# A decoder layer in FP32: the SyncE queue re-ordered, projections and the first output projection moved to other slices

## The chip, the cores and the metric

The kernel runs on one core of one Trainium2 chip. The metric is the device time of one execution in microseconds (us). A change of half a per cent is about what a measurement of this kernel can tell from none.

## What is computed

One pre-norm decoder layer, FP32, four batches of 512 tokens, hidden size 512. The attention has 32 query heads and 8 key and value heads of 16 columns; the feed-forward part has 1792 inner columns.

```python
def bitnet_linear(x, weight, scale_param):
    s = jnp.maximum(jnp.mean(jnp.abs(weight), axis=1), 1e-08)
    y = jnp.einsum('bsi,oi->bso', x, jnp.sign(weight / s[:, None])) * (s * scale_param)[None, None, :]
    return jnp.nan_to_num(y, nan=0.0, posinf=1000000.0, neginf=-1000000.0)
# attention: q, k, v = bitnet_linear(x, ...), softmax(q k^T / 4) v, then bitnet_linear(..., o_weight, o_scale)
# FFN weights: W = mean_w + mean(|w - mean_w|) * sign(w - mean_w);  h = silu(x W1^T) * (x W3^T);  h W2^T
x = x + attention(layernorm(x))
x = x + ffn(layernorm(x))
```

## The kernel before

Every engine has its program written out by hand, and the engines meet at semaphores only. FP32 accuracy comes from splitting each operand into a high and a low FP32R part. The work has three parts.

**Attention** (lines 1321 to 1328 for PE). There are 32 *groups*, one for each batch and key head, and each group has four *slices* (`kt`, 128 keys each), so a batch is 32 slices. One slice of PE (`pe_slice`) is four shifted score products (L1254, one for each query head of the group, 50 rows: 48 of split queries and 2 of the "shift", the row maxima taken off before the exponential), two plain score tiles (L1238) 14 tiles ahead whose row maxima DVE takes (`maxima`, L973), and the values product of the slice before (L1264). ACT takes the exponentials (L813). In slice 1 PE transposes the maxima of the next group (L1244), DVE splits them (`split_shift`, L981 and L983), and SP writes them by DMA into two rows of each half of that group's `q_slot` (`load_shift`, L436). The first product of the next group waits for that (`shift_in`, L1250).

**Work beside it.** Groups of batch b also make the queries, keys and values of batch b+1: token statistics (DVE L898), normalising (POOL L620), transposes (PE L1176), a split (POOL L628, L630), six *items* of eight matmuls (`project_item`, L1184 and L1185), scaling (ACT L747), guards for infinities (POOL L641, L642, DVE L942), a second split (POOL L650, L652) and the store to DRAM (SP `store_item`, L395 to L398). `beside` says which slice has which piece, and it takes a bank of the ring of three PSUM banks (`RING3`) that the shifted scores use. The 14 tiles of each FFN weight are also loaded (`load_difference`), subtracted on POOL (L658), signed on ACT and summed in absolute value on DVE (L1069), one tile each 8 slices.

**The queue of SP** sets when transfers start. `sp_group(g)` issues in this order: the item stores due, the load of group g+3 (`load_group`), the shift rows of group g+1, a tile of differences, tokens, and last the store of the values of group g-1. SP waits at the first instruction that isn't ready, with all others behind it. Before the loop SP stores batch 0's items, loads groups 0 to 2, writes the output factors to DRAM element by element (L423), waits for that, reads them back (L426), and then issues the shift rows of group 0.

**The last groups** hold batch 0's output projection: reciprocals of the softmax sums (L988) in group 28, the scaled attention output (L994) in group 30, its split (L998), and four tiles `project` (L1275, L1276) with `residual` on DVE (L1010 to L1023, eight instructions a tile) in slices 2 and 3 of group 30 and 0 and 1 of group 31. Then follow `second_norm` (L1028 to L1034), 14 tiles of weights (DVE L1100, PE L1339, ACT L839), and the FFN of the four batches, in which the output projections of batches 1 to 3 are interleaved.

## Time and profile before

| what | us |
|---|---|
| three runs, median (lowest to highest) | 1076.51 (1076.15 to 1081.52) |
| the profiled execution's own time | 1076.51 |
| its span, first to last instruction | 1074.7 |
| start of the attention loop on PE | 78.4 |
| end of its last values product | 536.9 |
| first weight transpose | 544.8 |
| first FFN matmul | 580.5 |
| PE busy in the span | 967.8 (90%) |
| DVE, ACT, POOL busy | 748.9, 520.1, 243.0 |

The page gives busy time for each engine. A wait row says which engine and line sat idle until which other one released it. PE is busy nearly all of the time, yet a PE that waits in a queue of matmuls can count as busy, so the waits and the timeline of a stage say more than the share.

### The profile page before, as it was taken

What the parts mean: (1) busy time and instruction counts of PE and PEld (TensorE: products, weight loads), DVE (VectorE), ACT (ScalarE), POOL (GpSimd) and SP (SyncE); (2) the same over time, 40 slices, a digit from 0 to 9 for tenths busy, and PEclk for the clock granted to TensorE, in tenths of its full rate; (3) what the DMA queues carried; (4) which work ended last, traced back from release to release, by engine and by line L of the source; (5) the groups of instructions that cost most, each with busy time, mean ns of one, the idle gap of its engine ahead of it and who ended that gap; (6) DMA issues with size and microseconds to landing.
All of it is one profiled execution on the core that took longest, in us unless ns stands there. A gap on an engine that the chain in (4) does not pass through costs nothing.

```text
span 1074.7 us, 14205 instructions
## 1 busy us (share of the span) xinstructions
PE 967.8 (90%) x4770; PEld 617.4 (57%) x4770; DVE 748.9 (70%) x1020; ACT 520.1 (48%) x957; POOL 243.0 (23%) x231
## 2 busy tenths in 40 slices
PE   3548997899889988997968999999999999999997
PEld 2413443244333443332456888888888888888886
DVE  5469776987788757996786457865588456864443
ACT  3407775887578756886556232233313332232221
POOL 2004573366517552200000110101101010011110
PEclk9758998999889987997889999999999999999999
DMA  4565456445545365524457100231002400040001
GB/s 155 143 136 162 149 179 202 127 127 172 174 138 150 103 195 153 146 67 142 138 171 235 60 1 1 79 112 49 0 0 87 152 0 0 14 143 1 0 0 39
DMA packets 82257, 110.24 MB, mean 103 GB/s; under 512 B 11040, under 2 KB 34592, under 8 KB 82208
## 3 DMA queue, kind: packets, MB, share of 16 engines
q1 hardware_dynamic: 80048, 108.04, 33.1%
q10 hardware_dynamic: 2160, 1.58, 0.5%
q8 instruction: 27, 0.44, 0.2%
q14 instruction: 22, 0.18, 0.1%
HBM read 76.29 MB, written 32.78 MB: 101 GB/s over the span
## 4 chain that ended last, share of the span: by engine, by line
PE 67%; DVE 15%; DMA 8%; SPq 6%; issue 2%; ACT 2%; POOL 0%; DVEq 0%
PE psum L1349 14%; PE psum L1350 14%; PE psum L1351 14%; DVE nmx L973 8%; PE psum L1254 6%; PE psum L1264 6%; PE psum L1238 3%; DMA q_slot<-shift 3%; SPq L436 2%; PE psum L1184 1%; DMA factors<-wstat 1%; PE psum L1185 1%; DMA q_stack<-q_lo 1%; PE psum L1275 1%; PE psum L1276 1%
## 5 line engine op out<-in xcount | busy, mean ns | idle before, releaser
L973 DVE TENSOR_REDUCE nmx<-psum 128x2 f32<-128x1024 f32 x256 | 301.9, 1216 | 94.8 <-PE psum L1238 94.6
L813 ACT ACTIVATE probs<-psum 128x512 f32<-128x512 f32 x512 | 273.5, 603 | 104.8 <-PE psum L1254 103.7
L1254 PE MATMUL psum<-q_slot,k_slot 50*128 50x512 f32 x512 | 173.5, 499 | 35.0 <-DMA q_slot<-shift 32.9
L1349 PE MATMUL psum<-fxh,wh 128*128 128x512 f32 x448 | 175.2, 391 | 2.2 <-DVE wl L1111 2.2
L1350 PE MATMUL psum<-fxl,wh 128*128 128x512 f32 x448 | 175.2, 391 | 0.0
L1351 PE MATMUL psum<-fxh,wl 128*128 128x512 f32 x448 | 174.8, 390 | 0.0
L1254 PEld LDWEIGHTS psum<-q_slot,k_slot 50*128 50x128 f32 x512 | 76.0, 197 | 156.4 <-ACT probs L813 92.4
L697 POOL CAST dh<-w2T 128x512 fp32r<-128x512 f32 (+1 forms) x56 | 51.0, 912 | 430.7 <-PE psum L1351 393.5
L1264 PE MATMUL psum<-probs,v_slot 128*32 128x512 f32 x1024 | 147.2, 649 | 0.7 <-ACT probs L813 0.7
L1238 PE MATMUL psum<-k_slot,q_slot 48*128 48x512 f32 x512 | 114.6, 469 | 22.1 <-DVE nmx L973 20.6
L1118 DVE TENSOR_TENSOR gate<-gate,psum 128x512 f32<-128x512 f32 x56 | 38.4, 686 | 133.6 <-PE psum L1351 131.3
L866 ACT ACTIVATE hh<-gate 128x512 fp32r<-128x512 f32 x56 | 35.4, 632 | 162.3 <-DVE gate L1118 162.3
L863 ACT ACTIVATE gate<-psum 128x512 f32<-128x512 f32 x56 | 33.5, 599 | 164.0 <-PE psum L1351 164.0
L1349 PEld LDWEIGHTS psum<-fxh,wh 128*128 128x128 f32 x448 | 84.5, 189 | 20.9 <-issue 2.9
L1351 PEld LDWEIGHTS psum<-fxh,wl 128*128 128x128 f32 x448 | 84.5, 189 | 17.7
L1350 PEld LDWEIGHTS psum<-fxl,wh 128*128 128x128 f32 x448 | 84.4, 188 | 17.6
L1238 PEld LDWEIGHTS psum<-k_slot,q_slot 48*128 48x128 f32 x512 | 57.7, 208 | 54.0 <-DVE nmx L973 44.4
L1349 PE MATMUL psum<-dh,hh 128*128 128x512 f32 x224 | 88.2, 394 | 0.1
L1350 PE MATMUL psum<-dl,hh 128*128 128x512 f32 x224 | 88.2, 394 | 0.0
L1351 PE MATMUL psum<-dh,hl 128*128 128x512 f32 x224 | 87.1, 389 | 0.0
L1120 DVE TENSOR_TENSOR hl<-gate,hh 128x512 fp32r<-128x512 f32 x56 | 38.8, 692 | 39.8 <-ACT hh L866 39.8
L658 POOL TENSOR_TENSOR stage<-stage 128x1536 f32<-128x1536 f32 x14 | 48.6, 3471 | 36.5 <-DMA stage<-in_L_ffn_mean_w_dram 36.5
(107 smaller groups left out, 1209.3 us busy)
## 6 DMA issues: line engine op xcount, KB each, us to landing
stage<-in_L_ffn_mean_w_dram SPq DMA_DIRECT2D x84, 256.0 KB, 4.6
q_slot<-q_stack SPq DMA_DIRECT2D x64, 192.0 KB, 4.4
stage<-in_L_ffn_w_dram SPq DMA_DIRECT2D x42, 256.0 KB, 3.1
q_stack<-q_hi SPq DMA_DIRECT2D x32, 256.0 KB
weighted_values<-u_sb SPq DMA_DIRECT2D x32, 256.0 KB, 5.1
k_slot<-k_stack SPq DMA_DIRECT2D x64, 96.0 KB, 4.4
xn<-_attn_hidden_states_dram SPq DMA_DIRECT2D x4, 1024.0 KB, 5.7
q_stack<-q_lo SPq DMA_DIRECT2D x16, 256.0 KB
```

What stands on the lines that cost most here:

```text
L658: nc.gpsimd.tensor_tensor(wn[e % 2][:], wn[e % 2][:], mn[e % 2][:], ALU.subtract).then_inc(fd_ok, 1)
L697: nc.gpsimd.tensor_copy(dh[parity][:], w2T[:, bass.ds(src, 1), :].rearrange("p o c -> p (o c)")).then_inc(dh_ok, 1)
L813: nc.scalar.activation(probs[kt][:, j, :], BANK[ring_bank(("score", g, kt, j))], ACT.Exp, scale=HEAD_DIM ** -0.5).then_inc(exp_ok, 1)
L973: v.tensor_reduce(column, pair, AX.X, ALU.max, negate=True).then_inc(s_max, 1)
L1118: v.tensor_tensor(gate[:], gate[:], BANK[UP], ALU.mult).then_inc(h_ok, 1)
L1120: v.tensor_tensor(hl[p][:], gate[:], hh[p][:].bitcast(FP32), ALU.subtract).then_inc(hl_ok, 1)
L1238: last = mm(BANK[2 * jj + h], q_slot[s][rows, jj, q * P:(q + 1) * P], k_slot[s][rows, :], start=True, stop=True)
L1254: mm(BANK[ring_bank(("score", g, kt, j))], k_slot[s][rows, kt * P:(kt + 1) * P], q_slot[s][rows, jj, :], start=True, stop=True).then_inc(t ...
L1264: last = mm(psum[32 * j:32 * j + 32, 6, :], v_slot[g % 2][:, kt, :], probs[kt][:, j, :], start=(kt == 0), stop=(kt == TT - 1))
L1349: mm(o, lhs_hi, rhs_hi, start=first, stop=False)
L1350: mm(o, lhs_hi, rhs_lo, start=False, stop=False)
L1351: return mm(o, lhs_lo, rhs_hi, start=False, stop=final)
```

## The change

- SP, in each group: the shift rows of group g+1 come first, then the load of group g+3, then the values of group g-1, then the item stores, tokens and differences. The shift rows of both halves go in one DMA for each part, two a group where there were four.
- SP, before the loop: the shift rows of group 0 stand right after the third item store; the load of group 2 and the last two item stores follow. The factors are written in group 3 and read back in group 5.
- Work of batch b+1: transposes in slices 0 to 3 (8 to 11 before), items in slices 5, 8, ... 20 (13, 15, ... 23 before), values in 24 (28). Statistics and normalising are made one batch earlier; those of batch 1 stand ahead of the loop. The transposed tokens go back into `xn`, so that the two `xT` buffers and ACT's wait for them are gone.
- Batch 0's output projection: SP loads its operands from group 24, DVE scales them in slices 10 to 15 of the last batch, and a PE tile stands in slices 16, 20, 24 and 28, in a ring bank. `residual` is cut in three pieces, in the three slices that follow. PE no longer waits for the weights' coefficient in the loop.
- POOL fills the value slots two groups ahead, with three slots where there were two.
- The sums of absolute differences stay on DVE.

```diff
-STATS_AT, AGGR_AT, NORM_AT, XT_AT, SPLIT_AT = 0, 4, 5, 8, 9
-ITEM_AT = tuple(13 + 2 * i for i in range(len(ITEMS)))
-GUARD_LAG, PRED_LAG = 1, 4
-VT_AT = 28
+XT_AT, SPLIT_AT, STATS_AT, AGGR_AT = 0, 1, 12, 16
+NORM_AT = (24, 26, 28, 30)
+ITEM_AT = tuple(5 + 3 * i for i in range(len(ITEMS)))
+GUARD_LAG, PRED_LAG = 1, 3
+VT_AT = 24
+INVERT_AT, ATTENDED_AT, PROJECT_AT, PROJECT_EVERY = 4, 10, 16, 4
...
+V_SLOTS = 3
...
-        xT = [sb(f"xT{p}", [P, SEQ]) for p in range(2)]
...
-    SUMS_STEP = (0, 3)
-    ATTENDED_STEP = (2, 0)
-    SPLIT_STEP = (2, 1)
-    MEANS_STEP = (2, 1)
-    PROJECT_STEPS = [(2, 2), (2, 3), (3, 0), (3, 1)]
+    TOTALS_SLICE, MEANS_SLICE, COEFF_SLICE = 119, 121, 122
...
         if b == BATCH:
-            return None
+            t = (at - PROJECT_AT) // PROJECT_EVERY
+            return ("project", t) if at in range(PROJECT_AT, SLICES, PROJECT_EVERY) else None
...
-        store_item(0, 3)
-        store_item(0, 4)
-        group_stored(2)
-        load_group(sp, 2, 2, slot_in[2])
-        sp.wait_ge(wstat_ok, 5)
-        sp.dma_start(fac_dram.rearrange("a w p -> p a w"), wstat[:, 3:5, :],
-                     allow_slow_non_contiguous=True).then_inc(fac_out, 16)
-        sp.wait_ge(fac_out, 16)
...
         def load_shift(g, s):
             for part, ready in enumerate((sh_hi, sh_lo)):
+                r = ROWS + part
                 sp.wait_ge(ready, g + 1)
-                for h in range(2):
-                    r = HALF * h + ROWS + part
-                    sp.dma_start(q_slot[s][r:r + 1].bitcast(FP32).rearrange("o j (t c) -> o (j t) c", c=P),
-                                 shift[s % 2][8 * h:8 * h + 8, part, :].bitcast(FP32)).then_inc(shift_in[s], 16)
+                sp.dma_start(q_slot[s][r:P:HALF].bitcast(FP32).rearrange("h j (t c) -> h (j t) c", c=P),
+                             shift[s % 2][:, part, :].bitcast(FP32)).then_inc(shift_in[s], 16)
...
         load_shift(0, 0)
+        group_stored(2)
+        load_group(sp, 2, 2, slot_in[2])
+        store_item(0, 3)
+        store_item(0, 4)
...
         def sp_group(g):
...
-            if b + 1 < BATCH:
-                for i in range(5):
-                    if at <= ITEM_AT[i] + 6 < at + 4:
-                        store_item(b + 1, i)
+            if g < LAST_G:
+                load_shift(g + 1, (s + 1) % 4)
             if g + 3 < GROUPS:
                 positive(sp, t_mm, 16 * g)
                 group_stored(g + 3)
                 load_group(sp, g + 3, (s + 3) % 4, slot_in[(s + 3) % 4])
-            if g < LAST_G:
-                load_shift(g + 1, (s + 1) % 4)
+            if g > 0:
+                store_values(g - 1, s + 3)
+            if b + 1 < BATCH:
+                for i in range(5):
+                    if at <= ITEM_AT[i] + PRED_LAG + 3 < at + 4:
+                        store_item(b + 1, i)
...
+            if g == 3:
+                load_factors()
+            if g == 5:
+                spread_factors()
-            if last and s == 0:
+            if b == BATCH - 1 and at == 0:
                 for p in range(2):
                     sp.wait_ge(u_out[p], 16 * KV_HEADS // 2)
                 load_sums(0)
+                sp.wait_ge(v_ok, BATCH)
                 load_batch(0)
-            if last and s == 1:
+            if b == BATCH - 1 and at == 4:
                 load_reciprocals(0)
...
         pool.wait_ge(v_ok, 1)
         fill_values(0)
         fill_values(1)
+        for t in range(TT):
+            norm_tokens(1, t)
...
-            if kt == 1 and 0 < g < LAST_G:
-                pool.wait_ge(pv_mm, 4 * g)
...
+            if kt == 2 and g + 2 < GROUPS:
+                positive(pool, pv_mm, 4 * g)
...
+            if b + 2 < BATCH and at in NORM_AT:
+                norm_tokens(b + 2, NORM_AT.index(at))
...
-                nc.scalar.activation(xT[kt % 2][:], BANK[bank], ACT.Copy).then_inc(xe_ok, 1)
+                nc.scalar.activation(xn[:, :, kt * P:(kt + 1) * P], BANK[bank].rearrange("p (t c) -> p t c", c=P),
+                                     ACT.Copy).then_inc(xe_ok, 1)
...
-            step = (g % 4, kt) if g >= GROUPS - 4 else None
-            if step == SUMS_STEP:
-                invert_sums(0)
-            if step == MEANS_STEP:
+            if b == BATCH - 1:
+                if at == INVERT_AT:
+                    invert_sums(0)
+                if ATTENDED_AT <= at < ATTENDED_AT + KT:
+                    attended(0, at - ATTENDED_AT)
+                if ATTENDED_AT + 2 <= at < ATTENDED_AT + 2 + KT:
+                    lo_attended(0, at - ATTENDED_AT - 2)
+                if PROJECT_AT <= at:
+                    t, part = divmod(at - PROJECT_AT, PROJECT_EVERY)
+                    if part == 2:
+                        guard_output(c_chain)
+                    if part == 3:
+                        add_output(0, t, c_chain)
...
+        for i in range(TT):
+            token_stats(1, i)
+        token_means(1)
         for nn in range(S_AHEAD):
             maxima(nn)
...
-            if step == MEANS_STEP:
+            if 4 * g + kt == MEANS_SLICE:
                 pe.wait_ge(dtot_ok, 1)
                 pe.wait_ge(s_max, S_USES)
                 mm(BANK[MEAN_BANK][:, 0:3], ones[:], dtot[:], start=True, stop=True).then_inc(ctot_mm, 1)
-                pe.wait_ge(coeff_ok, 1)
-            if step in PROJECT_STEPS:
-                project(0, PROJECT_STEPS.index(step))
```

SP's queue before the loop, before the change, from the load of group 2 on (`factors` is the slow store, `fac_row` what is read back, `q_slot<-shift` the shift rows):

```order
L324 DMA q_slot<-q_stack 48x2x512
L326 DMA k_slot<-k_stack 48x512
L324 DMA q_slot<-q_stack 48x2x512
L326 DMA k_slot<-k_stack 48x512
L423 DMA factors<-wstat 128x20x1
L426 DMA fac_row<-factors 128x2x512
L436 DMA q_slot<-shift 1x8x128 x4
```

and with it, from the third item's store on:

```order
L393 DMA q_stack<-q_hi 8x16x512
L394 DMA q_stack<-q_hi 8x16x512
L396 DMA q_stack<-q_lo 8x16x512
L435 DMA q_slot<-shift 2x8x128 x2
L319 DMA q_slot<-q_stack 48x2x512
L321 DMA k_slot<-k_stack 48x512
L319 DMA q_slot<-q_stack 48x2x512
L321 DMA k_slot<-k_stack 48x512
```

The shift rows now stand ahead of the load of group 2, and `factors` and `fac_row` have left this place.

SP's queue in group 5, before, from the two item stores to the shift rows of group 6 (`q_stack<-` are stores of items, `q_slot<-q_stack` and `k_slot<-k_stack` the load of group 8); the first row is still group 4's:

```order
L441 DMA weighted_values<-u_sb 128x512
L395 DMA q_stack<-q_hi 8x16x512
L396 DMA q_stack<-q_hi 8x16x512
L398 DMA q_stack<-q_lo 8x16x512
L395 DMA q_stack<-q_hi 8x16x512
L396 DMA q_stack<-q_hi 8x16x512
L398 DMA q_stack<-q_lo 8x16x512
L324 DMA q_slot<-q_stack 48x2x512
L326 DMA k_slot<-k_stack 48x512
L324 DMA q_slot<-q_stack 48x2x512
L326 DMA k_slot<-k_stack 48x512
L436 DMA q_slot<-shift 1x8x128 x4
```

and with the change, group 5 from its start:

```order
L435 DMA q_slot<-shift 2x8x128 x2
L319 DMA q_slot<-q_stack 48x2x512
L321 DMA k_slot<-k_stack 48x512
L319 DMA q_slot<-q_stack 48x2x512
L321 DMA k_slot<-k_stack 48x512
L440 DMA weighted_values<-u_sb 128x512
L393 DMA q_stack<-q_hi 8x16x512
L394 DMA q_stack<-q_hi 8x16x512
L396 DMA q_stack<-q_lo 8x16x512
L393 DMA q_stack<-q_hi 8x16x512
L394 DMA q_stack<-q_hi 8x16x512
L396 DMA q_stack<-q_lo 8x16x512
```

The shift rows stood behind ten DMAs of this group and now stand first, and the load of group 8 comes after them.

DVE around batch 0's first output tile, before (group 30; `oy` to `st` is one tile of `residual`):

```order
L998 TENSOR_TENSOR al<-an,ah 128x512 x4
L1010 TENSOR_TENSOR oy<-psum,fac_row 128x512
L1013 TENSOR_TENSOR o_alt<-oy 128x512
L1014 SCALAR_TENSOR_TENSOR o_alt<-o_alt,oy 128x512
L1015 TENSOR_SCALAR o_alt<-o_alt 128x512
L1016 SCALAR_TENSOR_TENSOR o_mask<-oy,fac_row 128x512
L1018 COPY_PREDICATED o_alt<-o_mask,oy 128x512
L1021 TENSOR_TENSOR x<-x,o_alt 128x512
L1023 BN_STATS st<-x 128x6
L1010 TENSOR_TENSOR oy<-psum,fac_row 128x512
```

and with the change (slices 16 to 19 of the last batch; `nmx` are row maxima):

```order
L980 TENSOR_REDUCE nmx<-psum 128x2 x2
L1019 TENSOR_TENSOR oy<-psum,fac_row 128x512
L980 TENSOR_REDUCE nmx<-psum 128x2 x2
L988 TENSOR_SCALAR shift<-psum 16x128
L990 SCALAR_TENSOR_TENSOR shift<-psum,shift 16x128
L980 TENSOR_REDUCE nmx<-psum 128x2 x2
L1025 TENSOR_TENSOR o_alt<-oy 128x512
L1026 SCALAR_TENSOR_TENSOR o_alt<-o_alt,oy 128x512
L1027 TENSOR_SCALAR o_alt<-o_alt 128x512
L1028 SCALAR_TENSOR_TENSOR o_mask<-oy,fac_row 128x512
L980 TENSOR_REDUCE nmx<-psum 128x2 x2
L1033 COPY_PREDICATED o_alt<-o_mask,oy 128x512
```

The tile's pieces now stand between the maxima of group 28, where there were no maxima left to take at the old place.

## Rows read from the trace of the kernel before

**Rows 1.** The page, part 2: granted TensorE clock in 40 slices, in tenths
```profile
PEclk9758998999889987997889999999999999999999
```

**Rows 2.** The page: chain that ended last, by line
```profile
PE psum L1349 14%; PE psum L1350 14%; PE psum L1351 14%; DVE nmx L973 8%; PE psum L1254 6%; PE psum L1264 6%; PE psum L1238 3%; DMA q_slot<-shift 3%; SPq L436 2%; PE psum L1184 1%; DMA factors<-wstat 1%; PE psum L1185 1%; DMA q_stack<-q_lo 1%; PE psum L1275 1%; PE psum L1276 1%
```

**Rows 3.** Waits of PE, then of SP: in all, times, longest
```profile
PE psum L1254 <- DMA q_slot<-shift: 32.9, 10, 10.2
...
SPq L395 <- POOL q_hi L650: 64.0, 9, 11.9
```

**Rows 4.** Windows by batch: us, then PE, PEld, DVE, ACT, POOL busy, clock, DMA
```profile
78.40:194.30 115.90, 103.02 (x581) 43.50 (x581) 91.75 (x107) 82.14 (x157) 57.22 (x46) 0.94 0.56 169
...
310.10:428.80 118.70, 107.07 (x592) 45.12 (x588) 92.00 (x108) 83.68 (x160) 57.44 (x47) 0.91 0.49 146
428.80:536.90 108.10, 99.77 (x538) 38.72 (x534) 89.35 (x110) 77.06 (x148) 8.53 (x9) 0.91 0.41 123
```

**Rows 5.** Timeline before the loop: start, us, engine, line, operation
```profile
53.17 10.28 DVE L973 TENSOR_REDUCE nmx<-psum 128x2 f32<-128x1024 f32 x9 [7.08 <-PE psum L1238]
...
63.36 0.27 DVE L981 TENSOR_SCALAR shift<-psum 16x128 fp32r<-16x128 f32 x1
...
60.16 0.56 SPq L423 DMA_DIRECT2D factors<-wstat  x1
...
67.39 0.80 PE L1238 MATMUL psum<-k_slot,q_slot 48*128 48x512 f32 x2 [0.34 <-DVE nmx L973]
78.43 0.79 PE L1254 MATMUL psum<-q_slot,k_slot 50*128 50x512 f32 x1 [10.24 <-DMA q_slot<-shift]
```

**Rows 6.** Timeline of SP and DVE in group 4
```profile
138.70 0.27 DVE L981 TENSOR_SCALAR shift<-psum 16x128 fp32r<-16x128 f32 x1
...
138.40 0.60 SPq L395 DMA_DIRECT2D k_stack<-q_hi  x1
...
143.13 2.72 SPq L436 DMA_DIRECT2D q_slot<-shift  x4
```

**Rows 7.** Timeline of DVE and PE, two quiet groups of batch 3
```profile
445.72 0.27 DVE L981 TENSOR_SCALAR shift<-psum 16x128 fp32r<-16x128 f32 x1
...
450.88 0.51 PE L1254 MATMUL psum<-q_slot,k_slot 50*128 50x512 f32 x2
...
451.66 2.36 DVE L973 TENSOR_REDUCE nmx<-psum 128x2 f32<-128x1024 f32 x2 [0.24 <-PE psum L1238]
...
467.77 0.27 DVE L981 TENSOR_SCALAR shift<-psum 16x128 fp32r<-16x128 f32 x1
```

**Rows 8.** Timeline of PE: one projection item, one transpose of tokens
```profile
145.15 0.50 PE L1184 MATMUL psum<-xh,signs_qkv 128*128 128x512 f32 x1
...
147.21 0.49 PE L1254 MATMUL psum<-q_slot,k_slot 50*128 50x512 f32 x1
...
220.93 0.66 PE L1176 MATMUL psum<-ident,xn 128*128 128x128 f32 x4
```

**Rows 9.** Timeline of DVE in the last groups: sums, then one output tile
```profile
486.81 0.95 DVE L988 RECIPROCAL sums<-sums 128x128 f32<-128x128 f32 x1 [2.63 <-DMA sums<-weighted_values]
...
518.06 0.69 DVE L1010 TENSOR_TENSOR oy<-psum,fac_row 128x512 f32<-128x512 f32 x1 [4.14 <-PE psum L1276]
...
523.61 0.69 DVE L1010 TENSOR_TENSOR oy<-psum,fac_row 128x512 f32<-128x512 f32 x1
```

**Rows 10.** Timeline after the loop
```profile
535.80 1.07 PE L1264 MATMUL psum<-probs,v_slot 128*32 128x512 f32 x8 [0.69 <-ACT probs L813]
...
542.04 1.91 DVE L1034 TENSOR_SCALAR an<-x,mv,rstd 128x512 f32<-128x512 f32 x4 [1.15 <-POOL rstd L689]
...
544.76 1.51 PE L1339 MATMUL psum<-ident,stage 128*128 128x128 f32 x6 [7.89 <-DVE stage L1100]
```

**Rows 11.** Chain around 76 us: start, us, what
```profile
76.47 1.92 DMA q_slot<-shift
```

**Rows 12.** The page, DMA issues: KB each, median us to landing
```profile
q_slot<-q_stack SPq DMA_DIRECT2D x64, 192.0 KB, 4.4
```

More of the change, by code:

```diff
@@ L412, in _ @@
         store_item(0, 1)
-        sp.wait_ge(slot_init, 10)
+        sp.wait_ge(slot_init, 8 + V_SLOTS)
         for g in range(2):
@@ L1003, in lo_norm, with scale_output, guard_output @@
                             ).then_inc(fxl_ok, 1)
-        def residual(b, t, chain):
-            row = [fac_row[:, a, :, :].rearrange("p t c -> p (t c)") for a in range(2)]
+        row = [fac_row[:, a, :, :].rearrange("p t c -> p (t c)") for a in range(2)]
+        def scale_output(b, t, bank):
+            if t == 0 and isinstance(b, int):
+                dve.wait_ge(fac_in, 16)
+            dve.wait_ge(o_mm, 4 * b + t + 1)
+            v.tensor_tensor(oy[:], BANK[bank], row[0], ALU.mult).then_inc(oy_ok, 1)
+            dve.wait_ge(oy_ok, 4 * b + t + 1)
+        def guard_output(chain):
             y = oy[:]
-            dve.wait_ge(o_mm, 4 * b + t + 1)
-            v.tensor_tensor(y, BANK[att_bank(b, t)], row[0], ALU.mult).then_inc(oy_ok, 1)
-            dve.wait_ge(oy_ok, 4 * b + t + 1)
             chain.link(v.tensor_tensor(o_alt[:], y, y, ALU.is_equal))
@@ L1023, in residual @@
             chain.link(v.bn_stats(st2[:, t, :], x1[:, t, :]))
+        def residual(b, t, chain):
+            scale_output(b, t, 6 + t % 2)
+            guard_output(chain)
+            add_output(b, t, chain)
         def second_norm(b, chain):
```

127 lines of the change are left out of this document (64 added, 63 removed).

## The prediction

> **What bounds the kernel now.** I read the page first, then the chain, the waits, the windows by batch, and last the timeline of each place that the change touches. By the chain, most of the time is PE's FFN matmuls (L1349 to L1351, over 40%), which this change leaves alone; behind them come DVE's maxima, the attention's matmuls and, at 3% and 2%, the DMA of the shift rows and SP's issue of it [rows 2]. So the whole gain has to come from the first 580 us. The waits give it a name: PE stood 32.9 us for the shift rows, at ten places, 10.2 us at one of them [rows 3]. In the clock row the reader is to see that the clock is not full in much of the first half, though it is in the FFN [rows 1]: a stalled PE is granted the lower of its two levels (1.2 in place of 2.4 GHz) for a while after.
>
> Where do the stalls come from? In group 4 DVE has split the maxima at 138.97, but SP was busy from 138.40 with the store of a key item, then the load of group 7, and issues the shift rows at 143.13, 4.2 us late [rows 6]. SP's wait for POOL's item splits, 64.0 us in all, is the same queue seen from the other side [rows 3].
>
> What a group costs without side work shows in batch 3: 22.05 us from one split of maxima to the second one after it, with one difference tile in them [rows 7]. DVE is busy 2.36 of each 2.61 us slice there and waits 0.24 for PE [rows 7], so the two are nearly balanced.
>
> **The change, term by term.** The sum is made against the profiled execution, whose own time is 1076.5 us, the median of the three runs too; 1.8 us of it lie outside the span.
>
> *1. Before the loop.* The ninth row maximum is followed by the split of group 0's maxima, done at 63.6, but PE starts only at 78.43, having waited 10.24 us [rows 5]. The shift rows stand behind the slow store of the factors, issued at 60.16 [rows 5]. With them first, two DMAs issued at some 0.7 us each and landing 1.92 us after the last issue begins [rows 11] are there by 66.4. PE is ready at 68.2, after its last score tile [rows 5]. **-10.2 us.** DVE's new work ahead (4 statistics and 5 small ones, 3.5 us) lies in the 7.08 us that it waits before its first maximum [rows 5]. POOL's normalising runs beside the score tiles. Both cost nothing here; if that cover were gone, 3.5 us would come back.
>
> *2. Batches 0 to 2.* Before, they take from 78.4 to 428.8, 350.4 us [rows 4]. I build up what such a batch needs with the shift rows on time: four pairs of groups at 22.05 make 88.2 [rows 7]; six items at 2.06 of PE make 12.4, four transposes at 0.6 make 2.4 [rows 8], the values' transpose about as much as one of these, 0.6. The statistics are 3.5 us of DVE in four or five slices, of which one has an item that hides them: 1.9, in batches 0 and 1 only, since batch 2 has none left to make. That is 105.5, 105.5 and 103.6, in sum 314.6. I add 3: the loop begins on the low clock as before, now with transposes in it, and the factors' store shares the DMA rings with group 4's transfers. That gives 317.6, and **-32.8 us**. Of this 22.7 are the nine waits inside the loop (32.9 less 10.2) [rows 3]; the other 10 are the low clock after them (0.94, 0.94 and 0.91 in the windows of rows that I read [rows 4]) and items that had to be guarded, selected and stored within four slices. Bounds: only the waits go and nothing else, -22.7; or the build-up holds without the 3, -36.
>
> What moves beside that and costs nothing: POOL's splits of the transposed tokens (4 of 1.9 us, and a difference of 3.5 us) have to be ready for PE's slice 5. Four slices of some 3 us and one of 2.7 hold them with 3 us to spare. The item stores wait for POOL two slices longer than before, but stand behind the shift rows, so that only the stores themselves are late, and the first group that reads them is loaded a group or more later. ACT's lost wait for `xT` was hidden.
>
> *3. Batch 3.* It takes 108.1 us [rows 4]. DVE is the bound where the output tiles now are. A tile of `residual` is 5.55 us, start to start [rows 9]; a group's maxima and split are four times 2.36 and 0.55, so groups 28 and 29 take 15.5 each where a quiet one takes 11: 31.1. Groups 24 to 27: two pairs, 44.1; the sums, 0.95 and a wait of 2.6 for them [rows 9]; eight scalings at 0.69, the time of the first operation of a tile [rows 9], 5.5; in sum 53.2. Groups 30 and 31 have eight slices, seven without maxima, at ACT's 2.2 each, two PE tiles of 2 us and 2 us of rest: 22. With 1.5 for the operands' loads, which come in a burst, it is 107.8. **0 us**: the tiles leave the end, but DVE pays for them earlier. Bounds: -6, if PE and ACT, not DVE, set the pace, and +8, if every piece falls where DVE is already late.
>
> *4. After the loop.* Before, the last values product ends at 536.9 and the first weight transpose starts at 544.76, after PE waited 7.89 us for DVE, which was still at `residual` and `second_norm` [rows 10]. Now the last tile on PE is in slice 28; 5.55 us of `residual`, 3.8 us of norm and one scaling later DVE is some 2.7 us behind the last product. **-5.2 us**; bounds -7.2 (PE waits for the last copy alone) and 0.
>
> Sum: -10.2 - 32.8 + 0 - 5.2 = -48.2, **1028.3 us**, and I take 1028.
>
> **Rivals.**
>
> *A. The load of a group becomes the wait.* `load_group` went behind the shift rows. In a quiet group it can be issued 1.4 us after the split and lands 4.4 us after each issue in the median, with 1.3 us between its first and last [rows 12]: 7.1 us after the split. The split ends 4.9 us before the next group's first product [rows 7], and PE's first use is 3 us into that group: 7.9 us. There is 0.8 us of room. If crowded rings take it 2 us longer in half of the 22 groups before batch 3's, 11 times 1.3 is 14, and with a store or two in the way 20: **1048**. Against it: these groups are 2 us longer by an item, and the load now stands ahead of the item stores and not behind them. 0.13.
>
> *B. DVE in the last batch.* The upper bound of term 3: the pieces delay the maxima, and `attended` waits for its operands, 8 us: **1036**. For it speaks that DVE has only 0.24 us of rest in a slice [rows 7]. 0.15.
>
> *C. The merged shift transfer is slow, and it comes out slower than before.* One DMA now has an outer dimension of 2 where it had 8 rows each. If its time from issue to landing grows with the rows that each leg carries, from 1.92 to four times that, 7.7 us [rows 11], the rows land 8.4 us after the split where 4.9 are there [rows 7]: 3.5 us late in each of 31 groups, 109 us, and **1137**. It decides from a landing of 4.2 us on; above 5.8 it eats the whole gain. Against it: a transfer of 4 KB that needs 1.92 us spends them on its way, hardly on rows. 0.03.
>
> The Trainium skill speaks for C: "DMA: Bandwidth & Descriptors", in its rules for kernel authors, says that an outermost dimension under 16 confines a DMA to at most that many engines, so two here. By that rule alone each of the two engines would carry eight rows; no row of the kernel before shows such a transfer, and the same page puts a fixed cost of about 2 us on a DMA, with which the 1.92 us agree.
>
> *D. The waits were hidden.* They go, but PE then waits for DVE's maxima in the same slices and only the start's gain and the tail's remain, 15 us: **1061**. Against it: in the first of the three batches DVE is busy 92 of 116 us [rows 4]. 0.01.
>
> **The numbers.** My own case 0.66 (its range 1020 to 1035), A 0.13, B 0.15, C 0.03, D 0.01, and 0.02 for C mixed with the rest so that it ends within 0.5% (5.4 us, about what a measurement of this kernel can tell from no change). The range reaches from 1017, the better bounds of terms 2 and 4 with part of that of term 3 (-3.2, -2, -6 from 1028), to 1047, most of A. Faster by more than that bound 0.95 (mine, A, B, D), the same 0.02, slower 0.03 (C).
>
> **What would show it.** Right: PE's first shifted product near 68 us; no wait for the shift rows over 1 us in batches 0 to 2; clock near 1.0 in those windows; loop windows of about 106, 106, 105 and 108 us; the first weight transpose 3 us behind the last values product; FFN unchanged at 494 us. Wrong: a wait of PE's L1238 for `q_slot<-q_stack` (A); DVE busy over 97% with PE waiting for `nmx` in the last batch and more than 112 us there (B); shift rows landing over 4 us after issue (C). A wait of PE for POOL's `xl` before the first item would break term 2.

## The result, and the profile after

The changed kernel takes **1050.1 us** (median of four, 1044.2 to 1053.6), the kernel before 1078.9 beside it: ratio 0.973, 95% interval 0.967 to 0.979. It is faster, but 22 us slower than the forecast and 3 us above its range. The profiled execution took 1053.6 us, span 1051.5; it was the slowest of the four.

Lines move: L1290 is now the shifted scores (L1254 before), L1274 the scores, L980 the maxima, L1381 to L1383 the FFN, L949 DVE's select of an item (`COPY_PREDICATED`), L668 GpSimd's weights' difference. The page: clock, and the chain by line.

```profile
PEclk9858999999899989689999999999999999999999
...
PE psum L1381 15%; PE psum L1382 15%; PE psum L1383 14%; PE psum L1311 1%; PE psum L1312 1%; DMA stage<-in_L_ffn_mean_w_dram 1%; PE psum L1300 1%; PE psum L1371 1%; PE psum L1290 1%; DVE stage L1133 1%; PE psum L1327 0%; ACT probs L820 0%; DVE fxl L1009 0%; DMA weighted_values<-u_sb 0%; DVE res L1164 0%
```

The clock still has low places, and the shift rows and SP's issue are gone from the top of the chain [rows 1, 2]. PE's waits (in all, times, longest):

```profile
PE psum L1274 <- DVE nmx L980: 24.1, 38, 3.2
...
PE psum L1290 <- DMA q_slot<-shift: 9.5, 4, 4.7
```

32.9 us of waits for shift rows became 9.5 [rows 3], and no wait for a group's operands stands among PE's longest. SP issued the rows of every group but one 0.03 us after DVE had split them; the one is group 1, 5.07 us late. Windows by batch, then the FFN with what leads to it (us, busy PE, PEld, DVE, ACT, POOL, clock, DMA share, GB/s):

```profile
67.90:183.60 115.70, 105.11 (x581) 44.87 (x578) 93.22 (x109) 82.36 (x157) 57.20 (x47) 0.93 0.67 187
183.60:293.60 110.00, 104.82 (x592) 43.95 (x588) 94.56 (x108) 82.83 (x160) 57.36 (x47) 0.95 0.58 167
293.60:402.60 109.00, 104.69 (x593) 44.43 (x590) 91.79 (x99) 82.62 (x160) 51.62 (x43) 0.95 0.55 159
402.60:521.50 118.90, 104.70 (x538) 39.77 (x534) 94.85 (x125) 77.54 (x148) 5.89 (x8) 0.87 0.39 114
521.50:1051.50 530.00, 517.34 (x2344) 421.72 (x2344) 333.20 (x504) 170.71 (x298) 53.64 (x59) 0.99 0.17 58
```

Against about 106, 106, 105 and 108 in the forecast, the four batches are 10, 4, 4 and 11 us too long. Two of the forecast's own signs are missing: three waits for shift rows in batches 0 to 2 are over 1 us, and the clock is 0.93 to 0.95 there, not near 1.0. The timeline has a cause at each place. First, batches 1 and 2: DVE, POOL and PE around slice 23 of batch 1 (start, us, engine, line).

```profile
263.81 3.40 DVE L949 COPY_PREDICATED g_alt<-g_mask,yq 128x512 f32<-128x512 int32 x1
...
263.18 3.45 POOL L668 TENSOR_TENSOR stage<-stage 128x1536 f32<-128x1536 f32 x1
...
268.37 0.80 PE L1274 MATMUL psum<-k_slot,q_slot 48*128 48x512 f32 x2 [3.17 <-DVE nmx L980]
```

A select that takes 0.72 to 0.76 us elsewhere took 3.40, and ended 0.6 us after GpSimd's subtraction had; PE waited 3.17 us for the maxima behind it. What that costs is in the clock (same columns as above):

```profile
264.80:268.40 3.60, 0.42 (x6) 0.03 (x2) 3.60 (x3) 1.09 (x2) 1.83 (x1) 0.89 0.61 201
268.40:276.80 8.40, 8.40 (x33) 3.12 (x33) 4.54 (x4) 4.45 (x8) 3.53 (x3) 0.50 0.35 132
```

A granted clock of 0.50 for 8.4 us after a stop of 3.6: PE is busy in all of them, at 1.2 GHz. The same happens in batch 2 (the select at 373.01 took 3.17 us). Then, in the last batch, DVE at the sums, and near the start PE at group 1; SP's row is the issue of that group's shift rows.

```profile
420.56 0.95 DVE L995 RECIPROCAL sums<-sums 128x128 f32<-128x128 f32 x1 [3.28 <-DMA sums<-weighted_values]
...
81.66 1.18 SPq L435 DMA_DIRECT2D q_slot<-shift  x2
...
88.49 0.79 PE L1290 MATMUL psum<-q_slot,k_slot 50*128 50x512 f32 x1 [4.70 <-DMA q_slot<-shift]
```

Group 1's split was done at 76.58; SP was issuing the loads of two differences until 81.6. The other waits for shift rows, 1.70, 1.43 and 1.67 us, stand before groups 6, 7 and 26, whose rows SP issued at once: they were late in landing. The start (the first two rows) and the tail went as forecast or better:

```profile
67.36 0.79 PE L1274 MATMUL psum<-k_slot,q_slot 48*128 48x512 f32 x2 [0.34 <-DVE nmx L980]
67.95 0.62 PE L1290 MATMUL psum<-q_slot,k_slot 50*128 50x512 f32 x1
...
522.22 1.53 PE L1371 MATMUL psum<-ident,stage 128*128 128x128 f32 x12 [0.72 <-DVE stage L1133]
```

### The profile page after: what moved, and what is told of

The parts are those of the page before. It is cut to its first block, busy times and chain, and to the rows that moved or that the text cites. A ratio compares the mean times of both kernels' runs of the same rounds, so it can differ in the third digit from the quotient of the medians.

```text
span 1051.5 us, 14134 instructions
## 1 busy us (share of the span) xinstructions
PE 971.4 (92%) x4770; PEld 616.7 (59%) x4770; DVE 753.1 (72%) x1020; ACT 518.7 (49%) x957; POOL 242.5 (23%) x232
## 4 chain that ended last, share of the span: by engine, by line
PE 49%; DVE 1%; DMA 1%; ACT 1%; issue 0%; SPq 0%; DVEq 0%; ACTq 0%
PE psum L1381 15%; PE psum L1382 15%; PE psum L1383 14%; PE psum L1311 1%; PE psum L1312 1%; DMA stage<-in_L_ffn_mean_w_dram 1%; PE psum L1300 1%; PE psum L1371 1%; PE psum L1290 1%; DVE stage L1133 1%; PE psum L1327 0%; ACT probs L820 0%; DVE fxl L1009 0%; DMA weighted_values<-u_sb 0%; DVE res L1164 0%
## 5 line engine op out<-in xcount | busy, mean ns | idle before, releaser
L980 DVE TENSOR_REDUCE nmx<-psum 128x2 f32<-128x1024 f32 x256 | 301.5, 1216 | 59.9 <-PE psum L1274 59.3
L1290 PE MATMUL psum<-q_slot,k_slot 50*128 50x512 f32 x512 | 173.8, 499 | 13.8 <-DMA q_slot<-shift 9.5
L1381 PE MATMUL psum<-fxh,wh 128*128 128x512 f32 x448 | 175.1, 391 | 2.2 <-DVE wl L1144 2.2
L1383 PE MATMUL psum<-fxh,wl 128*128 128x512 f32 x448 | 175.0, 391 | 0.0
L1290 PEld LDWEIGHTS psum<-q_slot,k_slot 50*128 50x128 f32 x512 | 76.1, 195 | 134.0 <-ACT probs L820 89.6
L1274 PE MATMUL psum<-k_slot,q_slot 48*128 48x512 f32 x512 | 113.5, 471 | 25.6 <-DVE nmx L980 24.1
L1381 PEld LDWEIGHTS psum<-fxh,wh 128*128 128x128 f32 x448 | 84.5, 189 | 20.8 <-issue 2.8
L1383 PEld LDWEIGHTS psum<-fxh,wl 128*128 128x128 f32 x448 | 84.5, 189 | 17.7
L1382 PEld LDWEIGHTS psum<-fxl,wh 128*128 128x128 f32 x448 | 84.4, 188 | 17.6
L1274 PEld LDWEIGHTS psum<-k_slot,q_slot 48*128 48x128 f32 x512 | 56.8, 207 | 58.7 <-DVE nmx L980 52.1
L1381 PE MATMUL psum<-dh,hh 128*128 128x512 f32 x224 | 88.2, 394 | 0.1
L1383 PE MATMUL psum<-dh,hl 128*128 128x512 f32 x224 | 87.1, 389 | 0.0
L1144 DVE TENSOR_TENSOR wl<-w3T,wh 128x512 fp32r<-128x512 f32 x56 | 56.1, 1002 | 0.0
```

What stands on the lines that cost most here:

```text
L980: v.tensor_reduce(column, pair, AX.X, ALU.max, negate=True).then_inc(s_max, 1)
L1144: v.tensor_tensor(wl[parity][:, k, :], w[:, bass.ds(src, 1), :].rearrange("p o c -> p (o c)"), wh[parity][:, k, :].bitcast(FP32), ALU.subt ...
L1274: last = mm(BANK[2 * jj + h], q_slot[s][rows, jj, q * P:(q + 1) * P], k_slot[s][rows, :], start=True, stop=True)
L1290: mm(BANK[ring_bank(("score", g, kt, j))], k_slot[s][rows, kt * P:(kt + 1) * P], q_slot[s][rows, jj, :], start=True, stop=True).then_inc(t ...
L1381: mm(o, lhs_hi, rhs_hi, start=first, stop=False)
L1382: mm(o, lhs_hi, rhs_lo, start=False, stop=False)
```

## The experiments

The length of a group is taken between the first shifted products of two groups in PE's timeline. Ratios are to the kernel before, measured beside it. Each run has one profile, and a place that an edit doesn't touch can differ between two profiles: e1_inv is the same program as the changed kernel up to batch 3, and its batch 0 took 122.4 us where that of the changed kernel took 115.7.

**1. One stall at a time.**

```diff
-INVERT_AT, ... = 4, 10, 16, 4          e1_inv
+INVERT_AT, ... = 6, 10, 16, 4
+                    if at == 25 and b + 1 < BATCH:          e2_gate
+                        pool.wait_ge(yg_ok, NI * (b + 2))
                     difference(e)
-        for e in range(2):          e3_late (and at the end of sp_group(0))
-            load_difference(e)
+        load_difference(0)
```

> The changed kernel, with the reciprocals of batch 0's sums two slices later (slice 6 of the last batch in place of 4), so that their DMA has two slices more to land. Theory (a stall costs itself and the low clock behind it): DVE's wait of 3.28 us before the reciprocal goes, PE's waits of 2.7 us for maxima in group 25 and of 1.67 us for group 26's shift rows go with it, group 25 takes 14 us in place of 18.6 and groups 26 and 27 gain 1 to 3 us more: 6 to 9 us less in the last batch, about 1043. Rival (the stall is only moved, the DMA lands late whatever the slice, or the output tiles take up the slack): the last batch stays within 2 us of 118.9 and the time within 3 us of 1050.

Measured: 1055.4 us, 0.976 (0.972 to 0.981). The theory fell. DVE no longer waits for the sums, but PE stops all the same, later and longer:

```profile
433.82 0.79 PE L1290 MATMUL psum<-q_slot,k_slot 50*128 50x512 f32 x1 [6.91 <-DMA q_slot<-shift]
```

SP's queue says why. Group 26's maxima were split at 421.5 and 421.8, while SP was still issuing batch 0's input and its values, behind the sums and a difference, 3.5 MB in all:

```profile
418.06 2.94 SPq L460 DMA_DIRECT2D sums<-weighted_values  x4
421.05 0.45 SPq L466 DMA_DIRECT2D x<-_attn_hidden_states_dram  x1
421.54 2.77 SPq L468 DMA_DIRECT2D an<-weighted_values  x4
424.35 1.15 SPq L435 DMA_DIRECT2D q_slot<-shift  x2
```

The wait for the sums had covered the wait for the shift rows: group 25 took 18.6 us in the changed kernel and 18.7 here.

> The changed kernel, with GpSimd holding its subtraction for the weights' difference at slice 25 of batches 0 to 2 until DVE's select of the last item (slice 23) is done. Theory: the select takes 0.75 us again in place of 3.40 and 3.17, PE's waits for maxima of 3.2 and 2.9 us at groups 14 and 22 go, these groups take 13 to 14 us in place of 17.8 and 17.6, and with the lower clock behind them 4 to 5 us go in each of batches 1 and 2: 8 to 10 us, about 1041. Rival (the select is slow for another reason, or GpSimd's later subtraction delays the items): the two groups stay over 17 us and the time within 3 us of 1050.

Measured: 1046.0 us, 0.969 (0.965 to 0.974). By place the theory holds, and more than it asked: groups 14 and 22 take 11.6 and 12.2 us in place of 17.8 and 17.6, and the batches' clocks are full:

```profile
188.90:292.70 103.80, 101.19 (x594) 42.36 (x590) 91.88 (x108) 82.41 (x160) 57.33 (x47) 1.00 0.60 176
292.70:395.90 103.20, 100.81 (x592) 42.51 (x588) 89.26 (x99) 82.14 (x160) 51.58 (x43) 1.00 0.58 167
```

The whole gained only 4 us by the medians, and the intervals of the two ratios overlap, less than the 12 that the two groups gained: batch 0 took 121.9 us in this profile, of which groups 4 to 6 were 45.8.

> The changed kernel, with the second weight difference's loads issued at the end of SyncE's work for group 0, behind group 1's shift rows, in place of ahead of the loop. Theory: group 1's shift rows are issued within 0.1 us of their split in place of 5.07 us late and land in 2 to 3 us in place of 6, PE's wait of 4.7 us in group 1 goes, and the first batch takes 109 to 112 us in place of 115.7: 4 to 6 us, about 1045. Rival (the 4.7 us are hidden behind DVE, whose maxima then are the wait, or the late loads hold up the second difference and GpSimd behind it): batch 0 stays over 114 us.

Measured: 1052.7 us, 0.974 (0.969 to 0.979). A miss: the shift rows are issued earlier, but the first difference's loads now land later, GpSimd waits 10.3 us for them and DVE, for its sums, behind it. Batch 0 took 122.9 us.

```profile
85.60 3.45 POOL L669 TENSOR_TENSOR stage<-stage 128x1536 f32<-128x1536 f32 x1 [10.29 <-DMA stage<-in_L_ffn_mean_w_dram]
...
89.08 0.69 DVE L1096 TENSOR_REDUCE dsum<-stage 128x1 f32<-128x512 f32 x1 [5.04 <-POOL stage L669]
```

> The three edits together. Theory (each stall costs itself and its clock, independently): the sum of the three, 18 to 25 us, so 1026 to 1032. Rival (another stall takes the place of each, DVE's work being the bound all along): under half of that, over 1040.

Measured: 1047.0 us, 0.971 (0.966 to 0.975): the rival's side. By place, the gate was a cure (batches 1 and 2 took 103.7 and 102.9 us); the other two moved a stall (batch 0 took 122.3, group 25 18.7).

**2. The rings**, the queues of the 16 DMA engines, whose busy share and GB/s end each window row. e5_burst moves `load_sums` right behind the shift rows and batch 0's input (1 MB) to group 27. e6_fac and e7_best:

```diff
-            sp.dma_start(fac_dram.rearrange("a w p -> p a w"), wstat[:, 3:5, :], ...)
+            for a in range(2):          e6_fac
+                sp.dma_start(fac_dram[a, OT:].rearrange("w p -> p w"), wstat[:, 3 + a, OT:], ...)
-DIFF_AT = tuple(range(1, 112, 8))
+DIFF_AT = (4,) + tuple(range(9, 112, 8))          e7_best, with e2, e3, e5 and e6
```

> The changed kernel, with the loads of the last batch spread: the sums are loaded right behind the shift rows of group 25, batch 0's input is loaded three groups later (group 27), the weights' difference and the values stay in group 24. The reciprocals stay at slice 4. Theory (the reciprocals two slices later gave nothing, since group 26's shift rows stood behind 3.5 MB of loads and SyncE's issue of them, and landed 9.5 us after the split): these rows land within 4 us of the split, DVE no longer waits 3.3 us for the sums, group 25 takes 12 to 14 us in place of 18.6, and the last batch 110 to 113 us in place of 118.9; the time 1042 to 1046. Rival (the output tiles on VectorE set the pace of the last batch): the last batch stays over 116 us, and the time within 3 us of 1050.

Measured: 1049.0 us, 0.974 (0.970 to 0.978). In the profile group 25 fell from 18.6 to 16.2 us and the last batch from 118.9 to 115.0, half of what was expected; the time shows nothing.

> The changed kernel, with the factors' store cut to what is read back, the four output tiles of each half: two DMAs with 1024 elements of 4 bytes in all, in place of one with 2560. Theory (in groups 4 to 6 the shift rows and operands stand in the rings behind that store, which took 18.3 us to land in the profile of the three edits together): it lands in 7 to 8 us, groups 4 to 6 take 38 to 41 us in place of the 44 to 46 of the three profiles that were slow there (41 in the changed kernel's own), and the time is 1044 to 1048 with less spread. Rival (it is the 0.5 MB broadcast behind it or the items' stores): groups 4 to 6 stay at 43 us or more.

Measured: 1057.3 us, 0.983 (0.980 to 0.986), some 7 us slower than the changed kernel where 2 to 6 less were expected, with *more* spread (1043 to 1063). The profiled execution is the fastest, 1043.1: there groups 4 to 6 took 40.0 us as expected. It also shows what the spread may be made of. At the place where the changed kernel lost 6 us, the same instructions here:

```profile
265.21 0.73 DVE L950 COPY_PREDICATED g_alt<-g_mask,yq 128x512 f32<-128x512 int32 x1
...
266.82 3.47 POOL L669 TENSOR_TENSOR stage<-stage 128x1536 f32<-128x1536 f32 x1 [2.22 <-DMA stage<-in_L_ffn_mean_w_dram]
```

The difference's weights landed late, so GpSimd began behind the select. Loads that land in time bring the collision, late ones avoid it. That the slower runs of this kernel are those with collisions is not shown: only one was profiled.

> All together: GpSimd held at slice 25 until the select is done, the loads of the last batch spread, the smaller factors' store, the second difference's loads behind group 1's shift rows, and the first difference on GpSimd at slice 4 in place of 1, so that its loads have landed. Theory (each stall costs itself and its clock): batch 0 takes 106 to 110 us, batches 1 and 2 103.7 and 103.3, the last 110 to 113: 1024 to 1032 in all. Rival (VectorE's output tiles hold the last batch, and the start-up transfers batch 0): over 1038.

Measured: 1036.5 us, 0.965 (0.962 to 0.967). Batches 0 to 3 took 112.4, 103.7, 103.0 and 118.1: the middle ones as expected, the outer ones not.

**3. Which half of the change does it?** e8_sp is the kernel before with `load_shift` moved to the top of `sp_group`; e9_order the changed kernel with item stores, group load, shift rows in the old order; e10_four the changed kernel with four DMAs for the shift rows.

> The kernel before, with one edit: SyncE takes the next group's shift rows first in every group, ahead of item stores and group loads; four small DMAs as before, all other work where it was, the start too. Theory (the waits for shift rows are SyncE's order): PE's wait for them falls from 32.9 us to under 15, of which 10.2 at the start, and the time from 1078 to 1050 to 1058; the rest of the change then brings the start's 10 us and little else, and its new stalls give back about as much as it wins in the batches. Rival (the spread of the projections is what lets the shift rows through, since a wait for GpSimd's splits stands in SyncE's queue whatever the order): the time stays over 1065.

Measured: **1108.4 us, 1.027 (1.025 to 1.030), slower than before.** The shift rows' waits in the loop are gone, as the first theory said (the 14.0 us are before the loop). The rival had the side, but neither size nor cause: it is another wait, for a group's operands, larger than the one removed.

```profile
PE psum L1238 <- DMA k_slot<-k_stack: 48.1, 12, 9.4
PE psum L1238 <- DVE nmx L973: 22.5, 37, 4.8
...
PE psum L1254 <- DMA q_slot<-shift: 14.0, 1, 14.0
```

Group 6 of that kernel and what follows it, POOL, SP and PE. An item's last part is split at 169.04 and could be stored. But SP has the shift rows first and stands, from 171.91 to 180.55, until DVE has split the maxima of the next group; the stores of this item and of the next follow at 183.31, the load of the group that reads them at 189.38, and PE, ready at 189.6, gets it at 198.93.

```profile
167.75 1.29 POOL L652 TENSOR_TENSOR q_lo<-g_alt,q_hi 128x512 fp32r<-128x512 f32 x1
...
171.49 0.42 SPq L441 DMA_DIRECT2D weighted_values<-u_sb  x1
...
183.31 0.60 SPq L395 DMA_DIRECT2D q_stack<-q_hi  x1
...
189.38 1.37 SPq L324 DMA_DIRECT2D q_slot<-q_stack  x1
...
198.93 1.22 PE L1238 MATMUL psum<-k_slot,q_slot 48*128 48x512 f32 x4 [9.32 <-DMA k_slot<-k_stack]
```

> The changed kernel, with SyncE's old order within a group: item stores, group load, then the next group's shift rows, then the values. Theory (the two halves of the change need each other: the shift rows first, alone, cost 32 us, since the operands then came late): without the new order PE's waits for shift rows come back, one for each group with an item whose parts GpSimd has not split when SyncE gets there, 15 to 25 us in the first three batches, and the time is 1062 to 1072. Rival (spreading the items alone does it, since fewer stores stand in a group): within 3 us of 1050.

Measured: 1058.3 us, 0.981 (0.975 to 0.987). PE's waits for shift rows:

```profile
PE psum L1290 <- DMA q_slot<-shift: 15.6, 5, 8.2
```

Less than the theory said: with the items three slices apart, SP reached the shift rows of groups 14 and 22 only 1.2 and 1.5 us late and those of group 5 3.6 us late; over half of the wait is group 1's, 8.2 us. So the order, which alone costs 30 us, adds some 8 to the rest of the change (the intervals just overlap), and the rest keeps some 21 of the 29 us without it. That rest is not the spread of the items alone: the start, the merged transfers and the new places of batch 0's projection are in it too, and no run has the spread by itself.

> The changed kernel, with the shift rows in four small DMAs as before in place of two merged ones. Theory (the merge saves SyncE two issues of some 0.5 us and changes nothing in the landing): the rows land some 1 us later after the split, hidden in most groups, since PE starts a group 4 us after it; the time 0 to 4 us over 1050. Rival (the merged transfer's two legs of eight rows were themselves slow, as the skill's rule on outer dimensions would have it): the rows land earlier by several us in the crowded groups, PE's 9.5 us of waits for them shrink to under 4, and the time is under 1043.

Measured: 1066.9 us, 0.989 (0.983 to 0.995), some 17 us slower than with the merged transfers, far more than expected. SP issues for 2.7 us in place of 1.1, and PE's waits for the rows double. Those of group 14 were issued right after their split and were used 8 us later, where in the changed kernel they were there within 4.9:

```profile
PE psum L1291 <- DMA q_slot<-shift: 19.2, 6, 7.6
...
271.33 2.73 SPq L436 DMA_DIRECT2D q_slot<-shift  x4
...
279.38 0.79 PE L1291 MATMUL psum<-q_slot,k_slot 50*128 50x512 f32 x1 [2.70 <-DMA q_slot<-shift]
```

The loads of a difference had been issued just ahead of them, so whether the four transfers are slow in themselves, or stand behind more, is open. In the profiles batch 0 holds 11.5 of the 13.6 us between the two kernels.

**4. The collision, made at will.** e11_force holds the same subtraction until the maxima of slice 22 are done.

```diff
+                    if at == 25 and b + 1 < BATCH:
+                        pool.wait_ge(s_max, 2 * (SLICES * b + 23) + S_AHEAD)
                     difference(e)
```

> The changed kernel, with GpSimd's subtraction of slice 25 held until VectorE has finished the maxima of slice 22 in batches 0 to 2, so that it always starts some 1.2 us before VectorE's select of slice 23. The profiles so far met the two together in some runs and batches and not in others (the select took 3.40 us in group 14 of one and 0.75 in two others of the same code there). Theory (a select waits for a running subtraction of GpSimd and gives PE a low clock behind it): the select takes 2.2 us or more in all three batches, groups 6, 14 and 22 take 14.5 to 18 us each in place of 11.6, and the time is 1054 to 1064. Rival (the slow selects had another cause): 0.75 us there and 1042 to 1050.

Measured: 1054.4 us, 0.977 (0.971 to 0.983). In batches 0 and 1 the select took 3.40 us and groups 6 and 14 17.8 and 16.3; in batch 2 the weights came 5.25 us late, GpSimd began at 382.00, behind the select, and it took 0.73. The time is at the low end of what the theory said, and its interval overlaps that of the changed kernel, but the places differ clearly. So the cause is shown, on and off, within one kernel:

```profile
162.97 3.40 DVE L951 COPY_PREDICATED g_alt<-g_mask,yq 128x512 f32<-128x512 int32 x1
...
162.32 3.46 POOL L668 TENSOR_TENSOR stage<-stage 128x1536 f32<-128x1536 f32 x1
...
380.55 0.73 DVE L951 COPY_PREDICATED g_alt<-g_mask,yq 128x512 f32<-128x512 int32 x1
...
382.00 3.46 POOL L668 TENSOR_TENSOR stage<-stage 128x1536 f32<-128x1536 f32 x1 [5.25 <-DMA stage<-in_L_ffn_mean_w_dram]
```

The profiles of all these kernels together say how the two meet. In 15 cases a select began while the subtraction ran, 0.4 to 3.0 us after its start; it took from 1.1 to 3.6 us, and in each of the 15 it ended 0.58 to 0.61 us after the subtraction had. In one case (e5_burst, batch 0) it began 0.07 us ahead of the subtraction, and took 0.74.

The Trainium skill has a rule for this: "SBUF — State Buffer", in the section "Who interferes with whom", says that a VectorE instruction with two inputs in SBUF contends with a GpSimd instruction that reads SBUF, and calls the contention an exclusive lock. The select has two such inputs, and the rows above agree. They agree only for the subtraction: in the kernel before, a select that began 0.5 us after a GpSimd operation with one tensor as its input, which reads SBUF too, took 0.80 us.

```profile
144.47 0.80 DVE L942 COPY_PREDICATED g_alt<-g_mask,yq 128x512 f32<-128x512 int32 x1
...
143.97 2.00 POOL L642 TENSOR_SCALAR g_mask<-yq,wstat 128x512 int32<-128x512 f32 x1
```

**5. The best version, and what is left of it.** e12_best2 is e7_best with the factors' spread in group 8 and the load of batch 0's values in group 25.

> The kernel with all edits together (1036.5), and two more transfers moved: the spread of the factors to group 8, where the rings are emptier, and the loads of batch 0's values behind group 26's shift rows in place of group 24. Theory (the last 5.8 us of PE's waits for shift rows and 1.4 for operands are full rings): they go, and with them 1 to 3 us each of low clock: 1028 to 1033. Rival (they are hidden behind VectorE, or meet other transfers): within 3 us of 1036.5.

Measured: **1034.7 us, 0.960 (0.956 to 0.965)**: within 3 us of 1036.5, the rival's side. The waits for shift rows did not go: they are 7.6 us, before groups 1, 5 and 27. The last batch took 112.9 us in place of 118.1, batch 0 took 115.1.

> The changed kernel with GpSimd's gate of the second experiment (so that no slow select mixes in), and the factors' store moved from group 3 to group 11, their spread from group 5 to group 13. Theory (the store's packets of 4 bytes fill the rings for 8 to 10 us, and group 5's shift rows stand behind them): groups 4 to 6 take 38 to 41 us in place of the 45.8 of the second experiment, and groups 12 to 14 take 43 to 47 in place of 37.4; the total stays within 3 us of 1046. Rival (batch 0 is slow there for another reason, such as differences loaded two at a time): groups 4 to 6 stay over 44 and groups 12 to 14 at 38.

Measured: 1040.9 us, 0.962 (0.957 to 0.968). Groups 4 to 6, then 12 to 14, in e2_gate and, second, in this kernel:

```profile
130.50:176.30 45.80, 39.47 (x222) 16.42 (x218) 34.92 (x43) 31.24 (x59) 25.26 (x18) 0.93 0.75 164
244.00:281.40 37.40, 36.04 (x221) 14.66 (x217) 33.73 (x42) 29.81 (x57) 25.22 (x18) 1.00 0.61 184
```

```profile
132.20:170.10 37.90, 36.51 (x222) 14.86 (x218) 34.27 (x43) 29.82 (x58) 25.27 (x18) 1.00 0.62 186
236.10:277.50 41.40, 36.53 (x222) 14.67 (x218) 34.93 (x43) 31.03 (x60) 25.24 (x18) 1.00 0.75 184
```

The stall follows the store: 7.9 us gone at the one place, 4.0 come at the other. The whole is 5 us under e2_gate's, where at most 3 were expected, but the intervals of the two ratios overlap. While the packets of 4 bytes are under way, the rings of e2_gate are this busy and carry this little (in the 4 us of the largest share; 0.63 to 0.65 in the 8 us that follow):

```profile
135.00:139.00 4.00, 4.00 (x25) 2.17 (x24) 2.80 (x6) 1.98 (x4) 2.83 (x3) 1.00 0.88 25
```

> The kernel of the twelfth experiment (1034.7), with the small factors' store issued right behind group 0's shift rows, ahead of the loop, without waiting there for it to land. Theory (the stall of groups 4 and 5 is that store, 5 to 6 us with its clock, and ahead of the loop the rings have room): groups 4 and 5 take 27.3 us in place of 31.0, batch 0 takes 108 to 111 in place of 115, and the time is 1028 to 1031. Rival (it only moves the stall to the shift rows of group 1 or the difference of slice 4): 1033 to 1038.

Measured: 1036.8 us, 0.961 (0.956 to 0.966). The rival's side: groups 4 and 5 take 26.5 us, but in group 0 PE waits for operands.

```profile
79.54 1.22 PE L1287 MATMUL psum<-k_slot,q_slot 48*128 48x512 f32 x4 [6.97 <-DMA k_slot<-k_stack]
```

> The kernel of the twelfth experiment, in which batch 0's output tiles are added without their guards: the four operations of the guard and the select are left out (3.2 us of VectorE for each of four tiles), for this batch alone. Theory (VectorE sets the pace of groups 28 to 30, PE waiting 1.2 and 0.6 us for maxima behind each tile): groups 28 to 30 take 34 to 38 us in place of 44.1 and the time is 1024 to 1028, since the last tile's guards are hidden in group 31. Rival (the projection's matmuls on PE and the lower clock set it): under 4 us less, over 1031.

Measured: 1028.2 us, 0.952 (0.947 to 0.956), 6.5 less than e12_best2. Groups 29 and 30, in e12_best2 and here:

```profile
455.20:486.30 31.10, 26.28 (x140) 10.43 (x136) 27.45 (x38) 18.29 (x34) 0.24 (x1) 0.95 0.15 49
```

```profile
455.10:480.50 25.40, 24.67 (x142) 10.33 (x138) 18.73 (x25) 17.83 (x34) 0.24 (x1) 1.00 0.21 61
```

5.7 us less, with 8.7 us less of DVE's work in them. From 439 us on, where e12_best2's PE waits 5.7 us in all for DVE's maxima, it waits for none here: DVE's guards set the pace there. Groups 28 to 30 took 40.8 us, not the 34 to 38 that were expected: the stretch from 434 to 447 us, in which group 28 begins, had a granted clock of 0.61. And the 6.5 us of the whole are not shown to be the guards': in the two profiles batch 3 took 112.9 and 113.2 us, since group 27 was longer, and the difference lies in batch 0 (115.1 and 109.8), which the edit does not touch.

## Why the prediction was wrong

Against the profiled execution the sum misses by 25 us, 1028.3 against 1053.6, and these are its parts. The forecast was of the median, which misses by 22.

*Term 1, the start: right.* 67.95 us was measured where 68.2 was forecast; statistics and normalising cost nothing.

*Term 2, batches 0 to 2: 334.7 in place of 317.6, 17 us.* The build-up itself held: with e2_gate's wait, batches 1 and 2 took 103.8 and 103.2, forecast 105.5 and 103.6. The step that failed is "what moves beside that and costs nothing". It asked whether GpSimd was in time, not what its subtraction does to DVE when both fall together. The new places put the last item's select in slice 23 beside the subtraction of slice 25, on which GpSimd starts early; groups 14 and 22 lost 6.3 and 6.0 us against 11.6, 12 together, some 3 of each as wait and as much again as low clock. The trace of the kernel before had a sign of it, a select of 1.09 us under a subtraction that was about to end:

```profile
175.60 1.09 DVE L942 COPY_PREDICATED g_alt<-g_mask,yq 128x512 f32<-128x512 int32 x1
...
172.60 3.47 POOL L658 TENSOR_TENSOR stage<-stage 128x1536 f32<-128x1536 f32 x1
```

Apart from that, batches 1 and 2 were 2 us under the forecast. The other 10 us are batch 0's, where I had allowed 3 for the low clock and the factors' store (12, less 2, plus 10, less 3, is 17). Its longest stall was 4.7 us for group 1's shift rows, which "first" in each group did not put ahead of the loads that stand before the loop; 1.7 and 1.4 us before groups 6 and 7 went to rows that were issued in time and landed late. The factors' store is a large part of that in other profiles (8 us, e13_move); how much of it this one has is not shown.

*Term 3, batch 3: +10.8 in place of 0, beyond its bound of +8.* Groups 24 to 27 took 59.2 us for 54.7: the "burst" for which I allowed 1.5 us is 3.5 MB ahead of group 26's shift rows (e1_inv); spread, these groups took 54.0 (e12_best2). Groups 28 and 29 took 30.1, forecast 31.1. Groups 30 and 31 took 29.5 where 22 was forecast. The sum itself was wrong there: eight slices at 2.2, two tiles at 2 and 2 of rest make 23.6, not 22. And its term was too small: I took ACT's 2.2 us for a slice, but in PE's timeline such a slice takes 2.6, as one with maxima does (four exponentials, 2.07, and a wait of 0.54 for PE's scores). With 2.6 the sum is 26.8; of the rest, 1.4 us are PE's waits for `oy`. That the guards are on the path of groups 29 and 30 is shown by e15_plain.

*Term 4, the tail: better.* PE waited 0.72 us where I had 2.7, and from the last values product to the first FFN matmul it is 35.9 us against 43.6 before: -7.7 for -5.2. The FFN took 494.2 us, unchanged.

With signs: -0.2, +17.1, +10.8, -2.5, in sum 25.2.

*Rivals.* **A**, the load of a group as the wait, had nothing to it in the changed kernel, and is what happens without the other half: 48.1 us in e8_sp. That its time of 1048 lies 2 us from the measured one is chance. **B**, DVE in the last batch, came in part, and not as its text had it: DVE was busy 94.85 of 118.9 us, not 97%, since its own waits stood between. **C**, a slow merged transfer: refuted, and turned round. With four transfers in their place the kernel took some 17 us more (e10_four). The Trainium skill's rule on an outermost dimension under 16 ("DMA: Bandwidth & Descriptors", rules for kernel authors) would confine each to two engines; whether it did, no row shows, and the trace puts no price on it. **D** is refuted by the result.

The range was too narrow on the high side: it let A stand for everything that could go wrong, and each of the three real losses (GpSimd's subtraction beside DVE, the loads ahead of the loop and the factors' store, the loads of the last batch in a burst) stood in it as covered or nearly so, at 0, 3 and 1.5 us.

## What to carry to other kernels

A reorder of one queue has a partner: putting a late consumer's transfer first makes everything behind it wait for that consumer's producer; alone it cost some 30 us here. Ask what stands behind the new first place, and try the halves alone. When an operation is moved beside another engine's, ask what both read at the same time, not only whether each is ready: here a subtraction that began 0.6 us ahead of a select cost 6 us. After a stall is cured, look at what it covered: behind DVE's wait for the sums (3.3 us) stood a wait for shift rows (6.9 us), and the group took as long as before.

## What was not expected of the hardware

- A select of 0.73 us on VectorE took 3.40 when GpSimd's subtraction of two SBUF tensors (3.45 us) had begun 0.65 us before it. In all 15 such meetings it ended 0.6 us after the subtraction had. Whether they meet can turn on when a DMA lands, so the same place in two batches of one profile differs by 5 to 7 us (e11_force).
- A stop of 3.6 us was followed by 8.4 us at a granted clock of 0.50; with it, the group was 6.2 us longer for a wait of 3.2.
- 10 KB stored in elements of 4 bytes took 14 to 19 us to land, and for 4 of them the rings were 0.88 busy at 25 GB/s; in e2_gate the shift rows issued 8 us behind it were used only 10 us after their issue. Cut to 4 KB in two DMAs, it still took 10 to 16.
- Two DMAs of 8 KB in place of four of 4 KB, for the same rows, were worth 17 us in 1050; SP's issue is 1.6 us shorter for each group, and how much of the 17 that makes, and how much the landing, is open.
